# Turning the normalised rows of a two-graph layer by DMA transposes of their f16 parts instead of TensorE transposes

## What is computed

```
xn  = An.T-mixed (adj @ x) + bias            # first graph layer, An from x itself
h   = layernorm(x + xn)                      # 128 rows of 512, over the 512
z_l = h @ W_lang.T ; z_g = h @ W_grav.T      # used only in products z z^T
A_l = relu(cosine of rows of z_l) ; A_g = exp(-distance of rows of z_g)
K   = w_l * rowstochastic(A_l * mask) + (1 - w_l) * rowstochastic(A_g * mask)
out = layernorm(h + K @ (h @ W_V.T) @ W_O.T)
```

## Time and profile before

| | us |
|---|---|
| median of 3 runs | 1049.05 |
| lowest, highest | 1045.99, 1049.55 |
| the profiled execution, its own time | 1050.14 |
| its span, first to last instruction | 1048.4 |
| one body in the steady part | 49.2 |

### The profile page before, as it was taken

How to read it: one execution, slowest core, us unless ns; L and a number is a source line. 1 busy time by engine, 2 the same in 40 slices (tenths; PEclk the granted TensorE clock), 3 DMA queues, 4 the chain that set the end, 5 groups by cost and what they waited for, 6 DMA issues and landing times.

```text
span 1048.4 us, 18878 instructions
## 1 busy us (share of the span) xinstructions
PE 961.5 (92%) x7052; PEld 571.7 (55%) x7052; DVE 809.7 (77%) x1659; ACT 506.3 (48%) x847; POOL 237.6 (23%) x295
## 2 busy tenths in 40 slices
PE   2899895756999999999999999999999999999994
PEld 2666593443646555555656564646555555556551
DVE  5999469983678878778778788787878778777776
ACT  5666336635345445454544545445445454544521
POOL 2666504423021120303030303021120303030300
PEclk9999997868899999999999999999999999999997
DMA  6442401011011111102011111111111112001011
GB/s 243 152 170 80 160 5 39 1 41 41 1 41 42 41 41 40 42 38 79 12 69 40 40 40 40 40 40 40 40 40 40 40 40 75 13 32 40 0 42 40
DMA packets 21967, 55.00 MB, mean 52 GB/s; under 512 B 1328, under 2 KB 1456, under 8 KB 19888
## 3 DMA queue, kind: packets, MB, share of 16 engines
q1 hardware_dynamic: 21936, 54.60, 14.3%
HBM read 37.82 MB, written 16.78 MB: 52 GB/s over the span
## 4 chain that ended last, share of the span: by engine, by line
PE 68%; DVE 16%; issue 9%; ACT 4%; POOL 1%; DMA 0%; DVEq 0%; ACTq 0%; POOLq 0%
PE bank L240 21%; PE bank L241 20%; PE bank L242 20%; DVE arena L1117 4%; ACT arena L889 3%; PE bank L609 3%; DVE arena L1067 2%; DVE arena L1085 2%; PE bank L661 1%; PE bank L635 1%; DVE arena L1451 1%; POOL arena L356 1%; DVE guess L1184 1%; PE bank L732 1%; DVE arena L1179 1%
## 5 line engine op out<-in xcount | busy, mean ns | idle before, releaser
L240 PE MATMUL bank<-arena 128*128 128x512 f16 (+2 forms) x1456 | 446.0, 324 | 10.6 <-DVE arena L1353 4.1
L241 PE MATMUL bank<-arena 128*128 128x512 f16 (+2 forms) x1456 | 444.8, 323 | 0.0
L242 PE MATMUL bank<-arena 128*128 128x512 f16 (+2 forms) x1456 | 443.4, 323 | 0.0
L240 PEld LDWEIGHTS bank<-arena 128*128 128x128 f16 x1456 | 142.9, 98 | 118.2 <-issue 11.7
L242 PEld LDWEIGHTS bank<-arena 128*128 128x128 f16 x1456 | 143.3, 98 | 111.6 <-issue 4.1
L241 PEld LDWEIGHTS bank<-arena 128*128 128x128 f16 x1456 | 143.1, 98 | 93.7 <-issue 2.6
L972 ACT ACTIVATE arena<-bank 128x512 f16<-128x512 f32 x128 | 76.3, 597 | 158.9 <-PE bank L242 157.3
L414 POOL TENSOR_TENSOR sq_parts<-cf,zero 128x4 bf16<-128x4 f32 x16 | 3.3, 208 | 572.3 <-DVE cf L1492 572.3
L1445 DVE SCALAR_TENSOR_TENSOR arena<-bank,arena 128x512 f16<-128x512 f32 x128 | 85.8, 687 | 44.5 <-ACT arena L972 44.5
L900 ACT ACTIVATE arena<-bank,bias_c,col 128x512 f32<-128x512 f32 x64 | 49.9, 780 | 102.7 <-PE bank L242 102.7
L398 POOL TENSOR_TENSOR arena<-arena 128x512 f32<-128x512 f32 x64 | 80.9, 1264 | 49.2 <-ACT arena L900 49.2
(11 more groups left out here) (265 smaller groups left out, 1558.3 us busy)
## 6 DMA issues: line engine op xcount, KB each, us to landing
arena<-in_x SPq DMA_DIRECT2D x32, 1024.0 KB, 5.3
out_dram<-arena SPq DMA_DIRECT2D x15, 1024.0 KB, 4.4
arena<-in_w_lang_t SPq DMA_DIRECT2D x1, 1024.0 KB, 5.2
arena<-in_w_grav_t SPq DMA_DIRECT2D x1, 1024.0 KB, 9.0
arena<-in_w_v SPq DMA_DIRECT2D x1, 1024.0 KB, 5.2
arena<-in_w_o_t SPq DMA_DIRECT2D x1, 1024.0 KB, 7.8
out_dram<-arena SPq DMA_DIRECT2D x4, 256.0 KB, 2.4
adj_sb<-in_adj SPq DMA_DIRECT2D x1, 64.0 KB, 14.3
```

The source lines that it names most:

```text
L240: pe.matmul(dst, ah, bh, start=start, stop=False)
L241: pe.matmul(dst, ah, bl, start=False, stop=False)
L242: return pe.matmul(dst, al, bh, start=False, stop=stop)
```

## The change

- TensorE's 16 transposes of h a group are gone (`turn_h`), with ACT's `hT_high` and DVE's `hT_low`, four of each a group.
- ACT's `first_norm` makes two outputs of y now: h in f32 and `h_h` in f16, by two activations of the same form. POOL makes `h_l = h - h_h` (`low_h`).
- SP issues a DMA transpose of `h_h` and one of `h_l` for each item, 8 a group, each 128 by 512 of f16, SBUF to SBUF (`turn_h` on SP). TensorE waits at the start of a body for all eight (`hT_in`).
- `hT_h` and `hT_l` exist twice, by slot; `h_h` and `h_l` exist once. `H_UP`, the scale of h's parts, is 1 instead of 256, with the other constants adapted.
- Mean and inverse deviation are worked out for items 0 and 1, then for 2 and 3: on DVE `first_moments` and `first_factors` run twice with half the columns, and on ACT `first_roots` runs twice.
- SP's loop is written out: `store(g-1)`, `turn_h(g+1)`, `load_x(g+3)`.

```diff
@@ sync
+            def turn_h(g, slot):
+                items = g * GB
+                done = items - GB
+                wait(sp, s["v_ps"], done)
+                for b in range(GB):
+                    item = items + (b + 1)
+                    sp.wait_ge(s["hh_ready"], item)
+                    sp.dma_start_transpose(hT_h[slot][:, :, b, :], h_h[:, b, :]).then_inc(s["hT_in"], 16)
+                    sp.wait_ge(s["hl_ready"], item)
+                    sp.dma_start_transpose(hT_l[slot][:, :, b, :], h_l[:, b, :]).then_inc(s["hT_in"], 16)
...
             load_x(2, 0)
+            turn_h(0, 0)
+            turn_h(1, 1)
             load_x(3, 1)
...
+            for g in range(1, NG):
+                store(g - 1)
+                if g + 1 < NG:
+                    turn_h(g + 1, (g + 1) % 2)
+                if g + 3 < NG:
+                    load_x(g + 3, (g + 1) % 2)
@@ gpsimd
+            def low_h(g, slot, b):
+                pool.wait_ge(s["h_ready"], g * GB + (b + 1))
+                pool.wait_ge(s["hh_ready"], g * GB + (b + 1))
+                pool.tensor_tensor(h_l[:, b, :], h[slot][:, b, :], h_h[:, b, :], ALU.subtract).then_inc(s["hl_ready"], 1)
...
                 if has_next:
                     residual(g + 1, 1 - slot, 3)
+                    for b in range(GB):
+                        low_h(g + 1, 1 - slot, b)
@@ tensor
-                pe.wait_ge(s["hT_l_ready"], g * GB + GB)
+                pe.wait_ge(s["hT_in"], g * TURNED + TURNED)
...
                 mm.then_inc(s["kT_ps"], 1)
                 if has_next:
-                    turn_h(g + 1, 1 - slot, 0)
-                    turn_h(g + 1, 1 - slot, 1)
-                    values(g, 3, False)
-                    turn_h(g + 1, 1 - slot, 2)
-                    turn_h(g + 1, 1 - slot, 3)
+                    values(g, slot, 3, False)
                 pe.wait_ge(s["kT_l_ready"], g + 1)
@@ scalar
+            def first_norm(g, slot, b):
+                act.wait_ge(s["ln1_ready"], g * 2 + (b // HALF + 1))
+                act.activation(h[slot][:, b, :], y[:, b, :], ACT.Identity, scale=ln1[:, 3, b:b + 1],
+                               bias=ln1[:, 4, b:b + 1]).then_inc(s["h_ready"], 1)
+                wait(act, s["hT_in"], g * TURNED)
+                act.activation(h_h[:, b, :], y[:, b, :], ACT.Identity, scale=ln1[:, 3, b:b + 1],
+                               bias=ln1[:, 4, b:b + 1]).then_inc(s["hh_ready"], 1)
@@ vector
                 if has_next:
                     first_stats(g + 1, 1)
+                    first_moments(g + 1, 0)
+                    first_factors(g + 1, 0)
                     first_stats(g + 1, 2)
...
                 if has_next:
                     first_stats(g + 1, 3)
-                    first_moments(g + 1)
+                    first_moments(g + 1, 1)
                 v_low(0)
                 if has_next:
-                    first_factors(g + 1)
+                    first_factors(g + 1, 1)
...
                 if has_next:
-                    hT_low(g + 1, 0)
-                    hT_low(g + 1, 1)
                     v_low(3)
-                    hT_low(g + 1, 2)
-                    hT_low(g + 1, 3)
```

More of the change, by code:

```diff
@@ L204, in build @@
         h = [at(32 * KIB, [GB, NODES]), at(40 * KIB, [GB, NODES])]
-        hT_h = at(48 * KIB, [KB, GB, P], F16)
-        hT_l = at(52 * KIB, [KB, GB, P], F16)
+        hT_h = [at(k * KIB, [KB, GB, P], F16) for k in (48, 160)]
+        hT_l = [at(k * KIB, [KB, GB, P], F16) for k in (52, 164)]
+        h_h = at(168 * KIB, [GB, NODES], F16)
+        h_l = at(172 * KIB, [GB, NODES], F16)
+        HALF = GB // 2
+        TURNED = 16 * 2 * GB
         z_h = [at(56 * KIB, [KB, GB, P], F16), at(64 * KIB, [KB, GB, P], F16)]
@@ L599, in mix_nodes, with project_z @@
                     mm.then_inc(s["mix_ps"], 1)
[L601 to L612, removed]
+            def project_z(g, slot, i, freed, done):
                 for n, e in enumerate(E_ORDER):
@@ L626, in half_products @@
                         mm = three(pe, bank[4 + i][:, b * P:(b + 1) * P], z_h[i][:, e, b, :], z_l[i][:, e, b, :],
-                                   hT_h[:, e, b, :], hT_l[:, e, b, :], start=(b == 0 and e == 0),
+                                   hT_h[slot][:, e, b, :], hT_l[slot][:, e, b, :], start=(b == 0 and e == 0),
                                    stop=(b == GB - 1 and e == KB - 1))
@@ L638, in add_turned, with values @@
                 mm.then_inc(done, 1)
-            def values(g, b, last_group, ks=range(KB)):
+            def values(g, slot, b, last_group, ks=range(KB)):
                 if ks[0] == 0:
@@ L647, in values @@
                 for k in ks:
-                    mm = three(pe, bank[b][:], hT_h[:, k, b, :], hT_l[:, k, b, :],
+                    mm = three(pe, bank[b][:], hT_h[slot][:, k, b, :], hT_l[slot][:, k, b, :],
                                w3_h[:, k, :], w3_l[:, k, :], start=(k == 0), stop=(k == KB - 1))
@@ L700, in body @@
                 else:
-                    between = lambda b, ks=range(KB): values(g, b, True, ks)
+                    between = lambda b, ks=range(KB): values(g, slot, b, True, ks)
                     pe.wait_ge(s["w_l_ready"], 7)
@@ L770, in _ @@
                 mix_nodes(0, b)
-            for b in range(GB):
-                turn_h(0, 0, b)
             pe.wait_ge(s["w_l_ready"], 6)
@@ L897, in add_bias @@
                 act.wait_ge(s["mix_ps"], g * GB + (b + 1))
-                wait(act, s["h_ready"], g * GB - GB + (b + 1) if not isinstance(g, int) or g > 0 else 0)
+                wait(act, s["hh_ready"], g * GB - GB + (b + 1) if not isinstance(g, int) or g > 0 else 0)
                 act.activation(y[:, b, :], bank[b][:], ACT.Identity, scale=c1(ALPHA_C),
@@ L954, in _, with first_roots @@
                 add_bias(0, b)
[L955 to L967, removed]
+            def first_roots(g, n):
+                act.wait_ge(s["ln1_var"], g * 2 + (n + 1))
+                mine = slice(n * HALF, (n + 1) * HALF)
+                act.activation(ln1[:, 1, mine], ln1[:, 0, mine], ACT.Ln).then_inc(s["ln1_log"], 1)
+                act.wait_ge(s["ln1_log"], g * 2 + (n + 1))
+                act.activation(ln1[:, 2, mine], ln1[:, 1, mine], ACT.Exp, scale=-0.5).then_inc(s["ln1_exp"], 1)
+            def first_norm(g, slot, b):
[5 more added lines that the diff above has]
+                               bias=ln1[:, 4, b:b + 1]).then_inc(s["hh_ready"], 1)
             def body(g, slot, has_next, has_second, has_previous, loads=0):
@@ L1574, in _ @@
                 first_stats(0, b)
-            first_moments(0)
-            first_factors(0)
-            for b in range(GB):
-                hT_low(0, b)
+            for n in range(2):
+                first_moments(0, n)
+            for n in range(2):
+                first_factors(0, n)
             x_low(1, 1)
```

90 lines of the change are left out of this document (47 added, 43 removed).

## The result

The changed kernel takes 1075.8 us (median of 4 runs, 1075.28 to 1076.27) beside 1049.3 of the kernel before: a ratio of 1.0259, with a 95% interval of 1.0238 to 1.0281. It is 2.6% slower. The time lies in the range that was given, but not on the side of the forecast, 1047, which was no change.

What follows compares the result with a forecast made beforehand. TensorE was taken as the bound: 1.75 us a body given back, 1.5 lost to `kT_l`, transposes hidden. 1050.14 minus 15 x 0.2 = 3.0, plus 1 at the start, is 1048.1; the median is 1.1 lower: 1047, range 1035 to 1125.

Steps and rivals of the forecast that it cites:

- TensorE as the bound, and the 1.75 us: Steady loop: TensorE sets the time; dropping its transposes of h gives back 1.75 us a body, 26.2 us over 15.
- The wait for kT: Ahead of `weighted` at a body's end: TensorE waits for `kT_l`, costing 1.5 of the 1.75 us; 0.2 is won.
- The DMA transposes: End of a body: the last transpose lands at 653.15, just ahead of TensorE's need at 653.35, so hidden.
- T: Queue time for one DMA transpose: bounds 0.38 and 2.65 us, taken as 1.0; at 1.07 the gain is gone.
- rival 1: Start of each body: transposes come late, T between 1.1 and 2; 1093 us at T = 1.5; chance 0.27.
- "slower": Whole kernel: a time above 1054.3 us, said to begin at T = 1.15 with 1055; chance 0.39.
- T = 5.2: Transpose queue: if blocks don't overlap, four at the page's 1309 ns each, giving some 1490 us.
- the low bound: SP's queue: T = 0.38 us for a transpose of 128 KB, since SP needs that to issue one.
- The rules of the Trainium skill: DMA transposes: one page has them as fast as regular DMAs, T 0.38; another 1309 ns for a 128 by 128 block.
- GpSimd against VectorE: First half's statistics: `low_h(0)` on GpSimd can hold up VectorE's L1536 or L1540 by about 0.4 us more.
- load_x, store: SP's queue: `load_x` waits for eight transposes with 13 us to spare, at no cost; `store` comes 20 us earlier.
- The start: First group: TensorE waits for its eight transposes; 3.5 us lost, 2.6 won back, 1 us in all.

Runs made afterwards that it cites:

- v_full: v_pair with item 1's norm, kT_h and kT_l moved earlier and GpSimd's low_h(1) held until VectorE made the factors: 1038.5 us, ratio 0.9916 to the kernel before.
- e_kt_first: Changed kernel with ScalarE's second and third v_high and kT_h put ahead of the norm of item 3: 1086.7 us, ratio 1.0359 to the kernel before.
- v_pair: Changed kernel with both parts of an item turned by one DMA transpose, four a group instead of eight: 1051.3 us, ratio 1.0045 to the kernel before.
- p_sizes: Kernel before with a tail on SP of DMA transposes of 128 to 2048 columns and plain copies: four of 128 columns took 5.02 us, four of 1024 5.38.
- e_norm1: Changed kernel with the norm of item 1 ahead of the second logarithm on ScalarE: 1057.3 us, ratio 1.0096 to the kernel before.
- e_whole: Changed kernel with the statistics back in one place and all four norms behind them: 1133.2 us, ratio 1.0831 to the kernel before.

## Why the prediction was wrong, point by point

**TensorE as the bound, and the 1.75 us**: right. With neither new wait in the way but one of 0.9, v_full loses just that and what surrounds it: 48.5 against 49.16 - 1.75 + 0.9 + 0.2.

**The wait for kT**: right in place, cause and size. Forecast 1.5, measured 1.61 idle, 1.77 in cost. The exponential ended at 657.18, 12.9 us being the shift between the two profiles: 644.3 on the old scale, against 643.85 to 644.2 forecast. The f16 norm takes 0.71 from start to start, as taken. In this kernel the wait didn't matter for the end, as the queue was later (e_kt_first); in v_pair it does.

**The DMA transposes**: this is the step that failed, by the size of its term T, the time of the queue for one transpose. It was taken as 1.0 us, where the transposes are just hidden; T is 1.31, over the 1.07 at which by the prediction the gain is gone, and over the 1.1 that it named as the sign of being wrong. Put into the same sum: the last starts at 645.4 + 6.55 = 651.95, lands at 655.0, 1.65 late; 1.45 net, 21.8 in 15 bodies, 3.5 at the start, 1074.3 against 1075.8 measured. So rival 1, to which 0.27 was given, is what happened, at the lower end of its T. Its reason, 512 small pieces, was wrong (p_sizes), and that its sum comes so near is in part luck: a transpose lands 2.5 us after its start, not 1.75 + 1.31 = 3.06, since SP's 1.3 and the landing overlap; against this `h_h(1)` was ready 0.3 later than taken, as `L1424` and `L1431` ran into GpSimd's `residual` and `k_g`, TensorE came to its wait 0.3 later as well, and 0.2 a body lies elsewhere. Two of the prediction's sums don't come out as printed: T = 1.15 gives 1059, not 1055, so "slower" begins just above 1.1; and T = 5.2 gives about 1540, not 1490. Neither changes the forecast.

**How T was taken**: the bounds were drawn from bytes and pieces, and what counts is a third thing, the time that SP's issue of a transpose takes. The issue row of a plain transfer, 0.38, was used as the low bound, and no row of before could show that a transpose costs more than three times as much to issue. The choice of a middle so near to the point where the sign turns should have moved more of the chances to the slower side than 0.39.

**The rules of the Trainium skill**: "Advanced Engine Details and Errata", X-Bar Transpose (TRN2), has transposing DMAs as fast as regular ones. The trace agrees nearly as to the landing, 2.45 us for one alone of 128 KB against 2.1 for a plain copy of the same size, and disagrees as to the queue, where the transpose takes 1.3 us of SP and the copy 0.6. Of "VectorE: DVE Perf Modes", The three transpose paths, the 1309 ns for a block of 128 by 128 agrees with the 1.3 us of SP for such an instruction, but not with a price for each block: four blocks, and eight, cost nearly the same.

**GpSimd against VectorE** was counted as a possible delay of 0.4; it was of that order in the changed kernel, and grew to the largest remaining cost once the queue was out of the way (0.57 in e_norm1, 0.9 in v_full). "GPSIMD Engine Reference" of the Trainium skill, Specifications, has the SBUF interfaces of GpSimd as shared with VectorE for instructions with two SBUF inputs or in a two-port mode; the steps of `k_mix`, with two SBUF inputs, agree with it, 1.14 to 2.04 us. The variance step, 0.17 to 0.74, has one, and no row shows in which mode it ran.

**load_x, store**: without cost, as said. **The start**: 1 forecast for T = 1.0, 3.5 by the same formula for 1.31, 3.3 measured.

What stays open: which part of SP's 1.3 us is spent on what, and why it jumps between 1024 and 2048 columns. What parts the six waits of e_kt_first behind which the clock was 0.50 from the nine others. And 0.1 to 0.3 us a body are in no wait that a view shows.

## What to carry to other kernels

A DMA transpose from SBUF to SBUF cost SP some 1.3 us here, whether it turned 32 KB or 256 KB: put everything that is ready together into one instruction, and count instructions in the queue, not bytes. When two waits follow one another, the earlier one may cost nothing, and taking it away can even cost: here it left one idle stretch of 2.5 to 3.0 us in place of two shorter ones, and behind 6 of 15 such stretches TensorE's granted clock was 0.50. Find the later one's chain first. Where a term of a sum has bounds far apart and the sign of the result turns inside them, the chances should follow the bounds and not the middle.

## What the hardware showed that was not expected

- SP's time for one DMA transpose: 1.3 us for 128 to 1024 columns of f16 on 128 partitions, 2.4 for 2048; landing 2.25, 2.45, 3.05 us after the start for 128, 512, 1024.
- TensorE, idle for 2.5 to 3.0 us in one piece once a body, came back at a granted clock of 0.50 for some 3 us in 6 of 15 bodies (e_kt_first), and with 2.9 and 2.4 us of idle time in every body (e_whole); with 1.6 and 1.2 us, in the changed kernel, it stayed at 1.00.
- A GpSimd subtraction of 1.2 us stretched a VectorE step of two columns from 0.17 to 0.74 us, and four steps of 128 by 128 from 1.14 to 2.04.
